# WO of a tile moved behind the next tile's QKV, the value product moved behind k's and q's transposes, k's rotary products moved between the reciprocals

## The reference

```python
h = shift_token(x)
q, k, v = split(h @ wqkv)              # 8 heads of 64
q, k = l2norm(q) * qs, l2norm(k) * ks
q, k = rotary_xpos(q, k)
sim = q k^T * 8                        # window 128: the own tile and the one before
attn = softmax(where(mask, -max, sim))
x = x + (attn @ v) @ wo
h = layernorm(shift_token(x)) @ w1     # h = a * gelu(g)
x = x + (a * gelu(g)) @ w2
```

## Time and profile before

| | us |
|---|---|
| median of 3 runs (2699.84 to 2702.57) | 2701.36 |
| the profiled execution | 2702.39 |
| its span, first to last instruction | 2700.6 |
| TensorE busy | 2542.8 (94%) |
| VectorE busy | 2075.8 (77%) |
| ScalarE busy | 1817.6 (67%) |
| POOL busy | 1483.8 (55%) |

### The profile page before, as it was taken

How to read it: one execution, slowest core, us unless ns; L and a number is a source line. 1 busy time by engine, 2 the same in 40 slices (tenths; PEclk the granted TensorE clock), 3 DMA queues, 4 the chain that set the end, 5 groups by cost and what they waited for, 6 DMA issues and landing times.

```text
span 2700.6 us, 81061 instructions
## 1 busy us (share of the span) xinstructions
PE 2542.8 (94%) x30176; PEld 2227.2 (82%) x30176; DVE 2075.8 (77%) x6597; ACT 1817.6 (67%) x5256; POOL 1483.8 (55%) x1767
## 2 busy tenths in 40 slices
PE   8999999999999999999999899999999999999998
PEld 7888888888888888888767788888888888888888
DVE  7878788777777777777656878777777788878876
ACT  6677777676676666766454767666676666666665
POOL 6565566555555565555213555655555565655654
PEclk9999999999999999999999999999999999999999
DMA  3122101003000000005100000000003100000000
...
DMA packets 75958, 82.25 MB, mean 30 GB/s; under 512 B 37552, under 2 KB 61872, under 8 KB 74416
## 3 DMA queue, kind: packets, MB, share of 16 engines
...
## 4 chain that ended last, share of the span: by engine, by line
DVE 37%; PE 29%; ACT 21%; issue 8%; DMA 3%; POOL 1%; SPq 1%; DVEq 0%; ACTq 0%; POOLq 0%
ACT pr L809 15%; PE bank L1101 7%; DVE t L1657 6%; DVE t L1654 6%; PE bank L1103 6%; PE bank L1102 5%; DVE t L1661 3%; DVE qT L1697 3%; DVE ssq L1668 3%; DMA stt<-stt 3%; DVE ssk L1668 2%; PE bank L1166 2%; PE bank L1486 2%; DVE oT L1703 2%; DVE pr L1681 2%
## 5 line engine op out<-in xcount | busy, mean ns | idle before, releaser
L627 POOL TENSOR_TENSOR pr<-pr,rden 128x384 f32<-128x384 f32 (+1 forms) x512 | 392.2, 782 | 530.4 <-DVE rden L1690 528.7
L809 ACT ACTIVATE pr<-pr,nb 128x192 f32<-128x192 f32 (+1 forms) x1024 | 438.2, 429 | 308.3 <-DVE nb L1681 308.3
L1101 PE MATMUL bank<-h2T,w 128*128 128x256 f32 x1408 | 402.6, 286 | 4.9 <-DVE h2T L1716 1.2
L1102 PE MATMUL bank<-h2T,w 128*128 128x256 f32 x1408 | 394.8, 280 | 0.0
L1103 PE MATMUL bank<-h2T,w 128*128 128x256 f32 x1408 | 394.6, 280 | 0.0
L1681 DVE CUSTOM_DVE_ANT_0 pr<-bank,maskb,r 128x192 f32<-128x192 f32 (+1 forms) x1024 | 348.4, 397 | 18.9 <-PE bank L1166 9.1
L659 POOL TENSOR_TENSOR uTl<-t,uTh 128x256 fp32r<-128x256 f32 x288 | 217.6, 756 | 213.1 <-ACT uTh L902 212.3
L1778 DVE SCALAR_TENSOR_TENSOR t<-bank,b,t 128x256 f32<-128x256 f32 (+1 forms) x384 | 183.0, 480 | 164.8 <-ACT t L887 104.5
L1101 PE MATMUL bank<-wqkv,hT 128*128 128x512 f32 x768 | 304.3, 396 | 2.1 <-DVE nb L1681 2.1
L1102 PE MATMUL bank<-wqkv,hT 128*128 128x512 f32 x768 | 302.2, 393 | 0.0
L1103 PE MATMUL bank<-wqkv,hT 128*128 128x512 f32 x768 | 300.6, 391 | 0.0
...
## 6 DMA issues: line engine op xcount, KB each, us to landing
...
stt<-stt SPq DMA_DIRECT2D x192, 0.0 KB
```

The lines of the kernel that those rows point to most:

```text
L627: e.tensor_tensor(probs(j, t), probs(j, t), rden[:, 2 * j:2 * j + 2].unsqueeze(2).to_broadcast([P, 2, w]), ALU.mult).then_inc(pn_done, 1)
L809: last = e.activation(probs(j, t)[:, g, :], probs(j, t)[:, g, :], ACT.Exp, bias=nb[:, hd:hd + 1], scale=-1.0, accum_out=den[:, hd:hd + 1])
L1101: e.matmul(out, left[0], right[0], start=first, stop=False)
L1102: e.matmul(out, left[0], right[1], start=False, stop=False)
```

## The change

In tiles 0 to 2, WO, its sum and its statistics move one tile on. On TensorE, WO(t-1) stands behind the QKV of tile t+1. The value product follows A0 and A2 and stands directly ahead of the next tile's scores (in tile 3 the rest of W2, H2T and WO(3) follow it). It is written to banks 6 and 4, PTE's transposes to bank 3. In tile 0, where there is no tile before, the value product is 8 matmuls over 128 rows in place of 16 over 64, each half of the heads in a bank of its own, and the sum `O_add` falls away. W2's units go to other places. On VectorE, in tiles 1 to 3, the two rotary products of k stand between the second and third reciprocal and its add between the third and fourth; ScalarE's square of k waits for the products. `LN_moments(0)` and POOL's `LN(0)` move from tile 2 to tile 3, and the four `LN_apply` of tile 3 behind everything of k and q.

```diff
--- before.py
+++ after.py
@@ -57,8 +57,8 @@
-E_BANK = 2
-O_BANK = (6, 3)
+E_BANK = 3
+O_BANK = (6, 4)
@@ -664,13 +668,13 @@
                     if prev and t:
                         XB(*prev, t)
                     for j in range(4):
+                        if t == 3 and j == 1:
+                            LN(L, b, 0)
                         NP(L, b, t, j)
                     if ahead:
                         A1(*ahead)
                     if prev and t == 0:
                         XB(*prev, t)
-                    if t == 2:
-                        LN(L, b, 0)
                     if L == 0 and t == 0 and b < B - 1:
                         entry_rstd(b + 1)
                 LN(L, b, 1)
...
@@ -828,21 +834,24 @@
                         last = e.activation(pTe[64 * a:64 * a + 64, g::2, :], halves_of[64 * g:64 * g + 64, :, a, :], ACT.Copy)
                 last.then_inc(pt_sb, 1)
-            def O_first(L, b, t):
+            def O(L, b, t):
                 n = idx(L, b, t)
-                e.wait_ge(o_lo, at(o_lo, 2 * n))
-                e.wait_ge(pv_ps, at(pv_ps, 2 * n + 2))
-                for i in pair:
-                    cols = slice(2 * P * i, 2 * P * i + 2 * P)
-                    e.activation(o_sum[:, cols], bank[O_BANK[0]][:, cols], ACT.Copy).then_inc(o_first, 1)
-
-            def O(L, b, t):
-                n = idx(L, b, t)
-                e.wait_ge(wo_ps, at(wo_ps, n))
-                for i in pair:
-                    e.wait_ge(o_added, at(o_added, 2 * n + i + 1))
-                    e.activation(oT[:, 0, 2 * i:2 * i + 2, :].rearrange("p a c -> p (a c)"), o_sum[:, 2 * P * i:2 * P * i + 2 * P], ACT.Copy).then_inc(o_hi, 1)
+                if t == 0:
+                    e.wait_ge(wo_ps, at(wo_ps, n))
+                    for i in pair:
+                        e.wait_ge(pv_ps, at(pv_ps, 2 * n + i + 1))
+                        e.activation(oT[:, 0, 2 * i:2 * i + 2, :].rearrange("p a c -> p (a c)"), bank[O_BANK[i]][:, 0:2 * P], ACT.Copy).then_inc(o_hi, 1)
+                else:
+                    e.wait_ge(o_lo, at(o_lo, 2 * n))
+                    e.wait_ge(pv_ps, at(pv_ps, 2 * n + 2))
+                    for i in pair:
+                        cols = slice(2 * P * i, 2 * P * i + 2 * P)
+                        e.activation(o_sum[:, cols], bank[O_BANK[0]][:, cols], ACT.Copy).then_inc(o_first, 1)
+                    e.wait_ge(wo_ps, at(wo_ps, n))
+                    for i in pair:
+                        e.wait_ge(o_added, at(o_added, sums(L, b, t) + i + 1))
+                        e.activation(oT[:, 0, 2 * i:2 * i + 2, :].rearrange("p a c -> p (a c)"), o_sum[:, 2 * P * i:2 * P * i + 2 * P], ACT.Copy).then_inc(o_hi, 1)
             def split_hi(i):
@@ -909,30 +918,31 @@
                 for t in range(NT):
                     ahead = (L, b, t + 1) if t < NT - 1 else nxt and (*nxt, 0)
                     ahead2 = (L, b, t + 2) if t < NT - 2 else nxt and (*nxt, t - 2)
+                    if t:
+                        O(L, b, t - 1)
                     for j in range(3):
                         S(L, b, t, j)
                     if t == 0:
                         A1_k(*ahead)
                     S(L, b, t, 3)
                     if ahead and t:
-                        A1_k(*ahead)
+                        A1_k(*ahead, True)
                     if ahead:
                         A1_qv(*ahead)
                     for a in pair:
                         PT(L, b, t, a)
                     if t:
                         PTE(L, b, t)
-                    O_first(L, b, t)
                     if ahead2:
                         A0(*ahead2)
-                    O(L, b, t)
-                    if t == 3:
-                        H2T(L, b, 0)
                     if ahead:
...
@@ -1147,8 +1157,6 @@
                 for j in banks:
                     if j == 2 and (t < NT - 1 or more):
                         e.wait_ge(ht_lo, at(ht_lo, n + 2))
-                    if j == 3:
-                        e.wait_ge(o_lo, at(o_lo, 2 * n))
                     if t == 0:
@@ -1173,6 +1181,8 @@
                 e.wait_ge(pn_done, at(pn_done, 4 * n + j + 1))
                 if j % 2 == 0:
                     e.wait_ge(pt_sb, at(pt_sb, 3 * n - 2 + a))
+                if j == 0:
+                    e.wait_ge(o_lo, at(o_lo, 2 * n))
                 if j == 0 and t == 0:
                     e.wait_ge(h2t_lo, at(h2t_lo, 2 * b + 16 * L))
                     if L == DEPTH and b == 0:
-                    e.wait_ge(v_sb, at(v_sb, n + 2))
+            def PTE(L, b, t):
                 for j in range(HEADS // 2):
                     mm = e.transpose(bank[E_BANK][:, j * P:(j + 1) * P], pr[:, j, P:2 * P], ident[:, :])
                 mm.then_inc(pt_ps, 1)
+            def PV_first(L, b, t):
+
+                n = idx(L, b, t)
+                e.wait_ge(xa_done, at(xa_done, n))
+                for j in range(HEADS // 2):
+                    if j % 2 == 0:
+                        e.wait_ge(pt_sb, at(pt_sb, 3 * n + j // 2 + 1))
+                    for g in range(2):
+                        hd = 2 * j + g
+                        mm = e.matmul(bank[O_BANK[j // 2]][64 * g:64 * g + 64, j % 2 * P:(j % 2 + 1) * P],
+                                      v[:, t, hd * DH:(hd + 1) * DH], pTm[:, hd, :], start=True, stop=True)
+                    if j % 2:
+                        mm.then_inc(pv_ps, 1)
+
             def PV(L, b, t):
+
                 n = idx(L, b, t)
                 e.wait_ge(xa_done, at(xa_done, n))
...
@@ -1233,7 +1253,9 @@
             def H2T(L, b, half):
                 done = 9 * b + (72 * L + 4 * half)
-                e.wait_ge(pt_sb, at(pt_sb, 3 * idx(L, b, 3) + 3))
+                if half == 0:
+                    e.wait_ge(pt_sb, at(pt_sb, 3 * idx(L, b, 3) + 3))
+                    e.wait_ge(o_added, at(o_added, sums(L, b, 3) + 2))
                 e.wait_ge(h2n_done, at(h2n_done, done + 1))
                 if half == 0:
                     e.matmul(bank[5][:, 0:2], pick[:, :], lead[:, :], start=True, stop=True)
@@ -1330,7 +1350,7 @@
                 for t in range(NT):
                     ahead = (L, b, t + 1) if t < NT - 1 else nxt and (*nxt, 0)
                     ahead2 = (L, b, t + 2) if t < NT - 2 else nxt and (*nxt, t - 2)
-                    cuts = ((5, 9, 12, 14, UNITS), (0, 6, 11, 14, UNITS), (0, 6, 11, 14, UNITS), (0, 6, 11, 11, UNITS))[t]
+                    cuts = ((5, 9, UNITS, UNITS), (0, 4, UNITS, UNITS), (0, 4, UNITS, UNITS), (0, 4, 8, UNITS))[t]
                     def fill(k):
                         if prev and cuts[k] < cuts[k + 1]:
@@ -1348,24 +1368,28 @@
                     else:
                         e.wait_ge(nb_done, at(nb_done, 4 * idx(L, b, t) + 1))
                         busy(14, 0)
+                    if t:
+                        WO(L, b, t - 1)
                     for j in range(4):
                         if not ahead and j > 1:
                             busy(4, 0)
                         PT(L, b, t, j, bool(nxt))
                     if t:
-                        PTE(L, b, t, bool(nxt))
+                        PTE(L, b, t)
                     fill(1)
-                    PV(L, b, t)
-                    if t == 3:
-                        H2T(L, b, 0)
                     if ahead2:
                         A0(*ahead2)
                     if ahead:
                         A2(*ahead, 0)
                         A2(*ahead, 1)
+                    if t:
+                        PV(L, b, t)
+                    else:
+                        PV_first(L, b, t)
                     fill(2)
-                    WO(L, b, t)
-                    fill(3)
+                    if t == 3:
+                        H2T(L, b, 0)
+                        WO(L, b, t)
                 for mt in range(MT):
                     W1(L, b, 0, mt, bool(nxt))
                     if mt == 2:
...
+            def rotary(L, b, t, i):
...
+                e.wait_ge((k_ps, q_ps)[i], at((k_ps, q_ps)[i], m + 1))
+                e.wait_ge((kt_ps, qt_ps)[i], at((kt_ps, qt_ps)[i], m))
+                e.tensor_tensor(t1[:, i, :].rearrange("p (h d) -> p h d", h=HEADS),
+                                bank[i][:, :].rearrange("p (h d) -> p h d", h=HEADS),
+                                rot[:, t, f:f + 1, :].to_broadcast([P, HEADS, DH]), ALU.mult)
+                e.tensor_tensor(heads(t2[:, i, :]), heads(bank[i][:, :])[:, :, ::-1, :],
+                                rot[:, t, f + 1:f + 2, :].to_broadcast([P, HEADS, DH]).rearrange("p h (c j) -> p h c j", c=2),
+                                ALU.mult).then_inc((rotk, rotq)[i], 1)
+            def rotated(L, b, t, i):
+                m = idx(L, b, t)
+                e.wait_ge((rotk, rotq)[i], at((rotk, rotq)[i], m + 1))
+                e.tensor_tensor((kr, qr)[i], t1[:, i, :], t2[:, i, :], ALU.add).then_inc((kr_step, qrot)[i], 1)
...
@@ -1881,8 +1915,14 @@
```

(55 more changed lines are left out.)

74 lines of the change are left out of this document (34 added, 40 removed).

## The result

The changed kernel takes 2737.72 us (median of 4 runs, 2735.22 to 2738.74) against 2700.74 for the kernel before beside it (2699.84 to 2702.57): ratio 1.0135, 95% interval [1.0117, 1.0152]. It is slower by 37 us; the forecast was 2728.

What follows compares the result with a forecast made beforehand. TensorE, busy 94%, was taken as the bound. Per sequence 11.7 + 14.0 + 14.4 + 19.0 + 18.4 = 77.5 against 76.59 us, 29 us over 32, 26 to 27 with a shorter tile 0: 2728 us, range 2655 to 2762.

Steps and rivals of the forecast that it cites:

- WO's wait goes: TensorE's wait before the WO product, for VectorE's oT, falls from 88.7 us to under 25.
- Tile 0, 11.7: Tile 0: next scores start at 11.7 us, 1.96 less than before, with the value product last at 0.95.
- Tile 1, 14.0: Tile 1: 13.72 us of TensorE work plus 0.3 waiting for k, 0.9 less than before.
- Tile 2, 14.4: Tile 2: scaled k comes 0.35 later, at 11.7, so the tile takes 14.4 us, 0.2 less than before.
- A0, A2 and value product at 2.96 together: TensorE in tiles 1 and 2: these three take 2.96 us of the 13.72, as in the kernel before.
- The port: Tiles 1 to 3: VectorE's add of k and POOL's normalisation exclude each other in SBUF, charged 0.61 us.
- The first rival: POOL is not held up by VectorE's add and late k is cheap: 45 us less, 2683; chance 0.2.
- Tile 3, WO's end at 19.0: Tile 3: POOL's queue delays k to 12.8 us, TensorE stands, and WO ends at 19.0 against 14.85.
- The stage, 18.4: Feed-forward stage: from WO's end to the next scores 18.4 us, against 18.57 before.
- the 1.2 that was named as a sign: End of tile 3: the first half's wait at H2T(1) would be near 1.2 us if the forecast is right.
- The SP queue "at nothing": Statistics DMAs of tiles 1 and 2, sent one tile later, and the load behind tile 2's in layer 0 cost nothing.

Runs made afterwards that it cites:

- the last kernel above: Changed kernel with tile 3's value product, LN's power, weight load and O_add reordered, plus tile 0's hT subtraction ahead of the W2 sum: 2649.92 us, 0.9803.
- run 16: Not a number: the run, 16 us under the changed kernel, with next layer's QKV weight loads ahead of tile 1's statistics DMAs: 2726.25 us, 1.0074.

## Why the prediction was right, and where it was not

The sign and the place were right: tiles 0 to 2 gain, tile 3 loses more than they gain together. The size (2737.7 for 2728) is near partly by luck: the usual sequences lose less than forecast, and the layer borders, counted at nothing, make up for it.

- *WO's wait goes.* Right.
- *Tile 0, 11.7*: 11.79.
- *Tile 1, 14.0*: 13.91, but not for the reason given. The forecast was 13.72 and 0.3 of waiting for k. TensorE does not wait for k in tile 1 at all. It waits 0.53 for hT in the second half of the scores (the row at 904.70 above), which the prediction did not have, and the work itself is shorter than 13.72 by what the next point says. k was as late as forecast, 11.4 for 11.3, and hidden by the wait for hT: in the last kernel above, where hT comes in time, tile 1 is 13.63 and the wait for k is there, 0.26 for 0.3:

```profile
884.21 1.09 PE L1157 MATMUL bank<-ident,t 128*128 128x128 f32 x8 [0.26 <-POOL t L622]
```

- *Tile 2, 14.4*: 13.99, 0.4 under the forecast. The late k was there, at 11.5 for 11.7, but the wait for it is 0.40, not 0.7. The term that was mis-sized is the A0, A2 and value product at 2.96 together: in tile 1, from A0 at 914.53 to the next scores at 917.14, they are 2.61. From the value product's start to the next scores are now 1.38 us, while in the kernel before the product ran from 841.24 to A0 at 843.08 (below), 1.84 us. There it stood ahead of A2, and its weight loads waited for ScalarE's copies (37.3 us in 96 waits in the list of the kernel before). I had looked for what the new order makes late, not for what A2 in front of the product covers. The run with the product first in tiles 1 and 2 prices the place from the other side, at 1.1 and 0.4 us a tile. The row of the kernel before:

```profile
843.08 0.44 PE L1113 MATMUL bank<-ident,Y 128*128 128x128 f32 x2
```

- *The port.* The third normalisation costs 0.44 to 0.45 more in the rows, where 0.61 was charged; the Trainium skill's rule (SBUF — State Buffer, "Who interferes with whom": the one that comes second waits out the whole instruction) fits the 0.68 for 0.24 and the 1.22 for 0.69 as well. It does not fit POOL's power over 128x8, beside which the add takes its usual 0.69 although it starts second; here the measurement decides. The first rival, 45 us from taking this conflict away, was wrong at its root. The add moved behind the squares met another POOL instruction, and k came no earlier. The products back behind the reciprocals did take the conflict out of tiles 1 and 2, and k came 0.77 earlier there, for 0.03 us a tile.
- *Tile 3, WO's end at 19.0*: 18.9, with k at 12.7 for 12.8 and a wait for it of 1.58, forecast as over 1.5. This was the core of the forecast, and two runs confirm its two halves. The power on POOL cost 23 of the 31 us expected. The value product with the chain of O behind it, standing behind the late k, cost 52, 1.7 us a sequence. The prediction wrote that k "is wanted with only the value product behind it", but did not ask whether the product needs k.
- *The stage, 18.4*: 18.6. H2T(1) waits 0.46, not the 1.2 that was named as a sign.
- *The SP queue "at nothing"*: wrong, and the largest single error. I looked for who waits for the moved DMAs, and at one load behind those of tile 2 in layer 0, but not at the load of the next layer's weights behind those of tile 1. By its run 16 us; the two sequences before a new layer alone are 14.5 us shorter in it.
- *The clock* was not in the forecast: 0.995 for 0.999. It costs the usual sequences nothing here: between 658.60 and 1200.00, and again between 1564.00 and 2020.00, the granted clock is 1.00, with a wait of 1.58 in the usual tile 3. The low stretches lie at the layer borders (0.59 over 8 us), in the third sequence and at the memory stage.

The errors partly cancel. The forecast had 0.9 us in each sequence, 29 us in all, and it is 0.72 in the usual one, 23 in all: the value product behind A2 is cheaper than charged, and the wait for hT takes part of that back. The two layer borders bring 14 us that were not in the forecast, most of them by the SP queue and at most 3.4 each by the clock. What is open: why moving LN's power is worth 23 us when k came 0.58 us earlier, which is 18 in 31 sequences (the two profiled executions differ by 15, so the noise of the ratios may be all of it), and why the clock falls in some sequences and not in others.
